# A mixture-of-experts stage: two of three f16 transposes a tile, done by DMAs from the Activation engine's queue instead of by TensorE

## The reference

```
xf = layernorm(x)
gate_scores = sigmoid(xf @ gate_w.T + balance_bias)          # 1024 tokens, 8 experts
topk_scores, topk_idx = top_k(gate_scores, 2)                # scores of the two, divided by their sum + 1e-6
h = silu(einsum('td,ehd->teh', xf, w1))                      # w1: 8 x 1024 x 512
expert_out = einsum('teh,edh->ted', h, w2)                   # w2: 8 x 512 x 1024
x = x + einsum('te,ted->td', comb, expert_out)
```

## Time and profile before

| | |
|---|---|
| median of 3 runs | 598.86 us |
| the profiled execution | 598.26 us, span 596.5 us |
| PE busy | 515.0 us, 86% |
| DVE busy | 401.4 us, 67% |
| ACT busy | 286.5 us, 48% |
| expert loop, first to last product | about 346.5 to 581.3 us of the span |
| DMA moved | 93.23 MB |

### The profile page before, as it was taken

The page is one execution under the profiler, slowest core; times in us unless marked ns, Lnnn a source line. Parts: engine busy times, 40 slices in busy tenths (PEclk is TensorE's granted clock), DMA queues, the critical chain, the costliest instruction groups (busy, mean ns, idle before and its releaser), DMA issues.

```text
span 596.5 us, 11365 instructions
## 1 busy us (share of the span) xinstructions
PE 515.0 (86%) x3769; PEld 304.1 (51%) x3770; DVE 401.4 (67%) x897; ACT 286.5 (48%) x449; POOL 114.8 (19%) x89
## 2 busy tenths in 40 slices
PE   5799999999989799886712799999999999999993
PEld 2674657475656576745401344554545555545451
DVE  2789778937978879688886656674664736673330
ACT  0662868676258374666610344562445426542120
POOL 1212114102241120300670011112111211121112
PEclk9889999999999999896855799999999999999997
DMA  8992505000008993144495157766472754623112
GB/s 320 391 382 75 213 1 212 2 1 2 1 1 324 381 381 132 37 142 142 177 316 200 46 199 210 231 185 196 123 240 36 243 145 132 220 53 53 35 35 35
DMA packets 32785, 93.23 MB, mean 156 GB/s; under 512 B 2896, under 2 KB 4080, under 8 KB 28656
## 3 DMA queue, kind: packets, MB, share of 16 engines
q1 hardware_dynamic: 23984, 74.81, 34.9%
q0 software_dynamic: 4304, 9.77, 8.2%
q10 hardware_dynamic: 4464, 8.22, 4.4%
HBM read 63.36 MB, written 29.43 MB: 156 GB/s over the span
## 4 chain that ended last, share of the span: by engine, by line
PE 67%; DVE 10%; issue 10%; ACT 5%; POOL 3%; DMA 3%; SPq 0%; ACTq 0%; POOLq 0%; DVEq 0%
PE bank L688 19%; PE bank L706 18%; PE bank L343 8%; PE bank L511 4%; PE bank L495 2%; PE bank L425 2%; PE bank L361 2%; PE bank L455 2%; PE bank L405 2%; PE bank L476 1%; PE bank L545 1%; ACT ctxT_region L736 1%; POOL small L1527 1%; DMA routed_rows<-shared,ints 1%; PE bank L604 1%
## 5 line engine op out<-in xcount | busy, mean ns | idle before, releaser
L688 PE MATMUL bank<-wbuf,ctx_region 128*128 x504 | 117.5, 392 | 6.5 <-issue 5.4
L1625 POOL DMA_INDIRECT out<-misc,ints x21 | 40.3, 1919 | 237.4 <-ACT misc L956 177.2
L688 PEld LDWEIGHTS bank<-wbuf,ctx_region 128*128 128x128 f16 x504 | 49.3, 100 | 66.9 <-issue 15.3
L1387 DVE SCALAR_TENSOR_TENSOR wbuf<-ctx_region,wbuf 128x2048 f32 (+1 forms) x28 | 62.9, 2288 | 25.9 <-ACT wbuf L875 25.9
L875 ACT ACTIVATE wbuf<-ctx_region 128x2048 f32 (+1 forms) x28 | 51.9, 1902 | 27.4 <-issue 25.6
L1527 POOL TENSOR_TENSOR small<-small 128x2 f32<-128x2 f32 (+2 forms) x25 | 27.7, 1109 | 189.2 <-DVE small L1017 182.6
L963 ACT ACTIVATE ctxT_region<-bank 128x512 f32<-128x512 f32 x42 | 25.1, 597 | 78.3 <-PE bank L688 78.3
L706 PE MATMUL bank<-wbuf,actT 128*128 x264 | 58.8, 379 | 1.0 <-DVE actT L1488 1.0
L706 PE MATMUL bank<-wbuf,xn 128*128 x240 | 53.4, 379 | 0.0
L511 PE MATMUL bank<-ctx_region,wbuf 128*128 128x256 f16 x384 | 43.3, 273 | 4.3 <-DVE ctx_region L1146 3.4
L1475 DVE COPY ints<-ctx_region 128x1 int32<-128x1 int32 x22 | 3.4, 154 | 61.0 <-PE bank L343 61.0
(11 more groups left out here) (214 smaller groups left out, 872.3 us busy)
## 6 DMA issues: line engine op xcount, KB each, us to landing
ctx_region<-in_experts SPq DMA_DIRECT2D x28, 1024.0 KB, 5.2
routed_rows<-ctxT_region SPq DMA_DIRECT2D x1, 16900.0 KB, 50.5
ctx_region<-in_ctx SPq DMA_DIRECT2D x8, 1536.0 KB, 9.1
ctx_region<-routed_rows ACTq DMA_DIRECT2D x23, 260.0 KB, 2.7
wbuf<-in_experts SPq DMA_DIRECT2D x4, 1024.0 KB, 4.8
out<-x ACTq DMA_DIRECT2D x8, 256.0 KB, 2.6
x<-in_x SPq DMA_DIRECT2D x1, 1536.0 KB, 14.5
wbuf<-in_wqT SPq DMA_DIRECT2D x4, 256.0 KB, 4.4
```

What stands on the lines that cost most here:

```text
L688: mm = nc.tensor.matmul(bank[half][:, :], xgT[:, b, x_part, k * P:(k + 1) * P], w16[:, ds(at + (w_part + k * EH + half * 512), 512)], star ...
L1387: nc.vector.scalar_tensor_tensor(w16[:, ds(at + (LOW + n * PIECE), PIECE)], src_[:, piece], W_SCALE, w16[:, ds(at + (HIGH + n * PIECE), PI ...
L1625: nc.gpsimd.indirect_dma_start(out, bass.IndirectOffsetOnAxis(idx[:, slot_no:slot_no + 1].bitcast(U32), axis=0), y_out[:, slot_no, :], Non ...
```

## The change

The rows of all tiles but the first, and the high hidden part of every tile, are transposed by DMAs with `transpose=True` from ACT's queue. Each takes 128 x 1024 f16 numbers (256 KB) from SBUF to SBUF, in eight blocks of 128 x 128. The low hidden part, and the rows of tile 0, stay on PE. PE's transposes of the rest go, with DVE's copy of the rows and ACT's copy of the high hidden part. New places and waits: ACT issues the DMA for the rows of tile u + 1 at the head of tile u, after a wait that its own rows have landed; it issues the DMA for the high hidden part right behind the two Silus, ahead of the weight cuts, after a wait for DVE's `h_hi`. DVE waits, before it writes the high part of a tile, until that of the tile before has landed in its transposed form (`hT0`).

```
 # PE
-            rows_T(0, 16)
-            first_product(0, 0, experts_of(0)[0])
-            rows_T(1, 16)
+            first_rows_T()
+            first_product(0, 0, experts_of(0)[0], first=True)
             hidden_T(0)
...
                     for u in (1, 2):
                         first_product(i * 2 + u, u % 2, experts[u])
-                        rows_T((u + 1) % 2, i * 16 + 32)
                         second_product(i * 2 + (u - 1), (u - 1) % 2, experts[u - 1])
                         hidden_T(i * 2 + u)
...
             def hidden_T(tile):
-                for part, cut, done in ((0, s["h_hi"], s["hT_ps0"]), (1, s["h_lo"], s["hT_ps1"])):
-                    pe.wait_ge(cut, tile + 1)
-                    transposes(bank[2 + part][:, :].bitcast(F16), [h16[:, part, k * P:(k + 1) * P] for k in range(HC)], done, ident16)
+                pe.wait_ge(s["h_lo"], tile + 1)
+                transposes(bank[3][:, :].bitcast(F16), [h16[:, 1, k * P:(k + 1) * P] for k in range(HC)], s["hT_ps1"], ident16)
 # ACT
+            def rows_T(b, landed):
+                act.wait_ge(xg_in[b], landed)
+                act.sem_inc(s["turning"], 1)
+                act.dma_start(xgT[:, b].rearrange("p a d -> p (a d)").rearrange("p (c t) -> p c t", t=P),
+                              xg16[:, b, 0:2 * D], transpose=True).then_inc(s["xgT"], 16)
+            def hidden(tile, b, landed, first=False):
+                if first:
+                    act.wait_ge(s["xgT0"], 1)
+                else:
+                    act.wait_ge(s["xgT"], tile * 16)
+                rows_T(1 - b, landed)
                 act.wait_ge(s["fields"], tile * 2 + 2)
                 load_rows(tile + 2, b)
...
-            def hidden_copy(tile, b):
-                act.wait_ge(s["hT_ps0"], tile + 1)
-                nc.scalar.copy(hT[b][:, 0, :], bank[2][:, :].bitcast(F16)).then_inc(s["hT0"], 1)
+            def hidden_T(tile, b):
+                act.wait_ge(s["h_hi"], tile + 1)
+                act.sem_inc(s["turning"], 1)
+                act.dma_start(hT[b][:, 0, :].rearrange("p (c t) -> p c t", t=P), h16[:, 0, :], transpose=True).then_inc(s["hT0"], 16)
...
                     for u in (1, 2):
-                        hidden(i * 2 + u, u % 2)
+                        hidden(i * 2 + u, u % 2, i * 16 + 32)
+                        hidden_T(i * 2 + u, u % 2)
                         cut_next_high(i * 2 + (u - 1), (2, 3))
                         cut_next_high(i * 2 + u, (0, 1))
-                        hidden_copy(i * 2 + u, u % 2)
                         gated(i * 2 + (u - 1), (u - 1) % 2)
 # DVE
-            def rows_copy(tile, b, again=True):
+            def rows_fields(tile, b, landed, again=True):
                 if again:
                     dve.wait_ge(s["idx"], tile - 1)
-                dve.wait_ge(s["xgT_ps"], tile + 1)
+                dve.wait_ge(xg_in[b], landed)
...
-                nc.vector.tensor_copy(xgT[:, b].rearrange("p a d -> p (a d)"), bank[(4, 7)[b]][:, :].bitcast(F16)).then_inc(s["xgT"], 1)
...
-            def cut_hidden(tile):
+            def cut_hidden(tile, again=True):
                 dve.wait_ge(s["h"], tile * 2 + 2)
+                if again:
+                    dve.wait_ge(s["hT0"], tile * 16)
                 nc.vector.tensor_copy(h16[:, 0, :], h).then_inc(s["h_hi"], 1)
```

More of the change, by code:

```diff
@@ L80 @@
 route rt_sel rt_cnt_ps rt_exp rt_slots rt_map zrow_fill zrow xs_zero rows_set scattered
-xg_in0 xg_in1 fields xgT_ps xgT h_ps h h_hi h_lo hT_ps0 hT_ps1 hT0 hT1 y2_ps y2 gate_parts gate idx scat added out_spare
+xg_in0 xg_in1 fields xgT_ps xgT0 xgT turning h_ps h h_hi h_lo hT_ps1 hT0 hT1 y2_ps y2 gate_parts gate idx scat added out_spare
 ident16 finished staged w_hi w1_lo w2_lo""".split()
@@ L668, in _, with first_rows_T @@
             pe.wait_ge(s["ident16"], 1)
-            def rows_T(b, landed):
-                pe.wait_ge(xg_in[b], landed)
-                transposes(bank[(4, 7)[b]][:, :].bitcast(F16), [xg16[:, b, k * P:(k + 1) * P] for k in range(2 * KC)],
+            def first_rows_T():
+                pe.wait_ge(xg_in[0], 16)
+                transposes(bank[4][:, :].bitcast(F16), [xg16[:, 0, k * P:(k + 1) * P] for k in range(2 * KC)],
                            s["xgT_ps"], ident16)
@@ L679, in experts_of, with first_product @@
                 return [(ready, ready % 2 * (2 * EXPERT)) for ready in (packed % 16, packed // 16 % 16, packed // 256)]
-            def first_product(tile, b, expert):
+            def first_product(tile, b, expert, first=False):
                 ready, at = expert
                 pe.wait_ge(s["w1_lo"], ready * 2)
-                pe.wait_ge(s["xgT"], tile + 1)
+                if first:
+                    pe.wait_ge(s["xgT0"], 1)
+                else:
+                    pe.wait_ge(s["xgT"], tile * 16)
                 for half in range(2):
@@ L701, in second_product @@
                 pe.wait_ge(s["w2_lo"], ready * 2)
-                pe.wait_ge(s["hT0"], tile + 1)
+                pe.wait_ge(s["hT0"], tile * 16 + 16)
                 pe.wait_ge(s["hT1"], tile + 1)
@@ L956, in gated @@
                 nc.scalar.activation(y_out[:, b, :], bank[5 + b][:, :], ACT.Copy, scale=gates[:, b, 2:3]).then_inc(s["y2"], 1)
-            def hidden(tile, b):
+            def rows_T(b, landed):
[4 more added lines that the diff above has]
+            def hidden(tile, b, landed, first=False):
+                if first:
+                    act.wait_ge(s["xgT0"], 1)
+                else:
+                    act.wait_ge(s["xgT"], tile * 16)
+                rows_T(1 - b, landed)
                 act.wait_ge(s["fields"], tile * 2 + 2)
@@ L980, in _ @@
             load_rows(1, 1)
-            hidden(0, 0)
-            hidden_copy(0, 0)
+            hidden(0, 0, 16, first=True)
+            hidden_T(0, 0)
             act.wait_ge(s["w2_lo"], 2)
@@ L1469, in cut_next_low, with first_rows_copy @@
                     cut_low(stage, at * -1 + 2 * EXPERT, pieces, ready * W_PIECES)
-            def rows_copy(tile, b, again=True):
+            def rows_fields(tile, b, landed, again=True):
                 if again:
                     dve.wait_ge(s["idx"], tile - 1)
-                dve.wait_ge(s["xgT_ps"], tile + 1)
+                dve.wait_ge(xg_in[b], landed)
                 nc.vector.tensor_copy(tokens[:, b:b + 1], xg[:, b, C_TOKEN:C_TOKEN + 1].bitcast(I32)).then_inc(s["fields"], 1)
                 nc.vector.tensor_copy(fields[:, b, :], xg[:, b, C_G1:C_E2 + 1]).then_inc(s["fields"], 1)
-                nc.vector.tensor_copy(xgT[:, b].rearrange("p a d -> p (a d)"), bank[(4, 7)[b]][:, :].bitcast(F16)).then_inc(s["xgT"], 1)
-            def cut_hidden(tile):
+            def first_rows_copy():
+                dve.wait_ge(s["xgT_ps"], 1)
+                nc.vector.tensor_copy(xgT[:, 0].rearrange("p a d -> p (a d)"), bank[4][:, :].bitcast(F16)).then_inc(s["xgT0"], 1)
+            def cut_hidden(tile, again=True):
                 dve.wait_ge(s["h"], tile * 2 + 2)
+                if again:
+                    dve.wait_ge(s["hT0"], tile * 16)
                 nc.vector.tensor_copy(h16[:, 0, :], h).then_inc(s["h_hi"], 1)
@@ L1503, in _ @@
             cut_low(expert0, 2 * EXPERT, (0, 1), 0)
-            rows_copy(0, 0, again=False)
+            first_rows_copy()
+            rows_fields(0, 0, 16, again=False)
             cut_low(expert0, 2 * EXPERT, (2, 3), 0)
-            rows_copy(1, 1, again=False)
-            cut_hidden(0)
+            rows_fields(1, 1, 16, again=False)
+            cut_hidden(0, again=False)
             hidden_copy(0, 0)
@@ L1514, in _ @@
                     for u in (1, 2):
-                        rows_copy(i * 2 + (u + 1), (u + 1) % 2)
+                        rows_fields(i * 2 + (u + 1), (u + 1) % 2, i * 16 + 32)
                         cut_hidden(i * 2 + u)
```

## The result

The changed kernel took 619.64 us (median of four runs, 617.79 to 630.49) beside 599.01 us (598.34 to 600.0) of the kernel before: a ratio of 1.033, with a 95% interval from 1.030 to 1.037. The forecast of 612 us had the direction right and was 7.6 us short; the time lies in the range of 590 to 690.

What follows compares the result with a forecast made beforehand. PE was taken to bound the expert loop end to end. Removing 23.5 us gave 575.4 us; 13 cut tiles at 0.8 + T, with T = 2.0, brought 612 us, 2% slower, range 590 to 690.

Steps and rivals of the forecast that it cites:

- What goes: PE, loop and ahead of it: row transposes 9.0, high hidden part 8.9, start 0.6, branch gap 5.0; 23.5 us less.
- The mechanism of the loss: ACT's queue in cut tiles: cast wait and DMA issue delay weight cuts, DVE's low copy and PE; 0.8 + T each.
- the formula: Total time: 575.4 + 13 x (0.8 + T) us, over the 13 of 20 tiles with weight cuts.
- T: Time one transposing DMA holds ACT's queue: taken as 2.0 us, range 0.34 to 5.3.
- Transfers: no cost: DMA engines in the loop: half busy, so two transposing DMAs a tile, 0.9 to 1.8 us each, fit at no cost.
- the third rival: Transposing DMAs fill all 16 DMA engines, up to 687 us; decides above 3.3 us each; chance 0.08.
- PE waits for the transfers themselves: Sign in the loop's changed profile that would show the predicted mechanism wrong; no size given.
- PE's clock at full: PE during the loop's new waits: full clock assumed, nothing added; a granted clock below 1 would add to them.
- Short issue: ACT's queue: the DMA's hold is short, 590 us at 0.34 us, faster below 1.0 us; chance 0.16.
- stronger form: ACT's table loads pass the wait for the cast, so all 23.5 us come, 575 us; chance 0.07.
- Long issue: ACT's queue bounds every tile when the hold exceeds 3.15 us; 685 us at 5.3; chance 0.17.
- Full DMA engines: Transposing DMAs keep all 16 engines 5.2 us each, 16.4 us a tile, 687 us; chance 0.08.

Runs made afterwards that it cites:

- E3: Changed kernel with only the rows transposed by DMA, both hidden parts on PE as before, old order on ACT: 588.32 us, ratio 0.988.
- E1: Changed kernel with the high hidden part's DMA issued behind ACT's table loads and weight cuts instead of ahead: 582.58 us, ratio 0.976.
- E9: E1 with only ACT's wait for DVE's cast put back ahead of the table loads and cuts: 592.5 us, ratio 0.990.
- E2: Changed kernel with both transposing DMAs as plain copies of the same bytes, same waits, expert outputs not the reference's: 598.47 us, ratio 1.0005.
- E4: Changed kernel with only the high hidden part by DMA, ahead of the cuts, rows back on PE and DVE: 615.65 us, ratio 1.035.
- E8: Changed kernel with each 1 MB weight piece loaded by four DMAs of 256 KB: 613.57 us, ratio 1.026.
- E10: Changed kernel with the high hidden part's DMA split into two of 128 x 512, both ahead of the cuts: 626.59 us, ratio 1.050.
- E6: E1 with the low hidden part also transposed by a DMA behind the cuts: 577.42 us, ratio 0.966.

## Why the prediction was right, and where it was not

**What goes: right.** Tiles without cuts run at 10.81 us, the forecast's 10.8; the gap at the branch closed; and E3, in which nothing new bound, came out at 588.3 us, where its half of the forecast gives 589.3. Ahead of the loop the forecast had 0.6 us, and about half of it came: from the start of the stage's first product to that of the next it took 13.39 us (324.82 to 338.21), now 13.12 (326.24 to 339.36). DVE's cast does follow the Silu at once now, but PE's idle time of the reason "issue" ahead of that product rose from 1.68 us to 2.04. And the first product began 1.4 us later in the profiled run, which was not in the sum.

**The mechanism of the loss: right.** The wait for the cast, the table loads that lose their cover, the cuts, DVE's copy: E1 undoes it and gains 35 to 37 us, E9 shows the wait's share, and E9, E2 and the changed kernel show the formula's slope in T. Its constant of 0.8 measured 1.07; ACT's cut began 3.11 us behind the DMA in the tile shown, where 2.88 was put in.

**T: mis-sized.** Taken as 2.0, it measured 1.27. The value was chosen midway between a plain issue's 1.20 and a backlogged queue's 2.92; the lower neighbour was nearly exact. With 1.27 the forecast's own formula gives 575.4 + 13 x 2.07 = 602.3 us.

**"Transfers: no cost": the step that failed.** It rested on plain transfers. Queue 10 and the packets of the loop, before and then after (345 to 600 us; packets, MB, share of 16 engines):

```profile
q10 hardware_dynamic: 2736, 5.06, 6.7%
```

```profile
DMA packets 49420, 44.44 MB, mean 174 GB/s; under 512 B 41589, under 2 KB 41589, under 8 KB 46453
q10 hardware_dynamic: 43333, 15.15, 37.6%
q1 hardware_dynamic: 3347, 24.27, 31.5%
```

The 39 transposing DMAs of that stretch added 10.1 MB in 40,600 packets, some 250 bytes each. They took 30.9% of 255 us, 2.0 us of all engines apiece: only just over the 1.8 that I had as the upper bound, and far from the 3.3 at which the third rival decides. The room had been read off a mean. The DMA share of the kernel before was 0.50 over the loop, but 0.68 in the first five cut tiles and 0.23 behind the last one; the changed kernel reaches 1.13 in a cut tile (same columns as above, before and then after):

```profile
345.00:408.00 63.00, 62.15 (x383) 31.95 (x382) 43.22 (x65) 32.69 (x31) 10.60 (x5) 1.00 0.68 211
536.00:580.00 44.00, 43.57 (x273) 22.52 (x272) 14.77 (x37) 9.22 (x15) 4.94 (x4) 1.00 0.23 42
```

```profile
526.00:537.00 11.00, 9.40 (x51) 4.39 (x50) 6.37 (x8) 5.48 (x5) 2.63 (x1) 1.00 1.13 193
```

Nor had I asked how long one takes to land beside weight loads: 3.1 us at best, up to 15.3. Three second products waited for one, 10.6 us, and "PE waits for the transfers themselves" was a sign that I had named of a wrong mechanism: it holds for these three of the thirteen waits. DVE's cast waited for the same three landings, 7.8 us, where the prediction saw about 9 us of room.

**PE's clock at full: the second step that failed.** Three second products in the PE timeline,

```profile
360.61 7.04 PE L708 MATMUL bank<-wbuf,xn 128*128 x24 [2.40 <-DVE xn L1507]
...
376.43 8.28 PE L708 MATMUL bank<-wbuf,actT 128*128 x24 [3.16 <-DMA actT<-ctxT_region]
...
421.12 8.12 PE L708 MATMUL bank<-wbuf,xn 128*128 x24 [6.41 <-DMA xn<-ctxT_region]
```

took 7.4 us more than three of 5.35, at a mean granted clock of 0.77, 0.62 and 0.64 in their windows (the two levels are 1.0, which is 2.4 GHz, and 0.5); the prediction named this and put it at nothing. PE had stood idle for 2.4, 3.2 and 6.4 us before them. It is no matter of landings alone: 1.7 of the 7.4 us stand behind a wait for DVE, and in E4 and E8, where no product waits for a landing, all of the 7.9 and 9.5 us do. Other waits of that size were not followed by it, as the one of 3.52 us above.

The account of the profiled execution, 620.3 us: 575.4; thirteen waits 34.3; lower clock 7.4; later start 1.4; 1.8 is not accounted for, of which some 0.3 is what did not come ahead of the loop. Against the formula at the measured T (602.3), the waits for DVE were 3.0 longer (10 x 0.3), the three for landings 4.4 longer than three times 2.07, and the rest as above: 18.0. So two errors of opposite sign, 9.5 us too much for T and 18 too little for landings, clock and start, gave 612. The hit is better than its reasons.

**The rivals.** Short issue: refuted by T, though its point of decision, T = 1.0, was only 0.27 us away. Its stronger form, loads that pass the wait: refuted by the 7.92 us of ACT's idle time. Long issue: refuted, 2.07 us was the longest in the changed kernel. Full DMA engines: refuted as a bound on every tile, by 2.0 us apiece where it needed 3.3 and by a pace of 10.81 us in tiles without cuts. In cut tiles it was not far off, as the share of 1.13 shows. Of the two pages that I set against each other: the figure of 1309 ns for a 128 x 128 block ("VectorE: DVE Perf Modes", "The three transpose paths", in the Trainium skill; the page gives it for bf16, not for f16) does not add up over blocks here, for eight f16 blocks land in 3.1 us at best. The other page ("Advanced Engine Details and Errata", "X-Bar Transpose (TRN2)", in the Trainium skill) says that transposing DMAs are as fast as regular ones. That does not carry over to what binds here: the queue is held 1.27 us against 0.48 for the same copy in E2, and in the loop only the transposing form made PE wait for a landing.

## What to carry to other kernels

Moving work off the bounding engine is half a change; the other half is where in the new engine's in-order queue its wait and its issue stand. Put them behind the work that others wait for (E1: one line, some 36 us), and count the hold per DMA, not per block (E10). Before calling a transfer free, ask when it must land and what else is then in the DMA engines, in the very tiles in which it must land; a mean share over the stage (0.50 here) doesn't tell. And where a change makes PE wait, price the clock too: in E8 slow products cost 9.5 us beside waits of 29.3.

## What the runs showed of the hardware

- In the changed kernel a transposing DMA of 128 x 1024 f16 from SBUF to SBUF held ACT's queue 1.26 to 1.29 us (medians). One of 128 x 512 held it 1.29 to 1.30 (E10), a plain copy of 128 x 1024 0.48 (E2), a plain row load from DRAM 0.35. Issued right behind another one, it held it 2.2 to 2.3 (E6).
- It moves in packets of about 250 bytes, lands in 3.1 us at best and in up to 15.3 beside 1 MB weight loads, in up to 8.9 beside the same loads cut in four (E8).
- In a cut tile of the changed kernel the DMA engines moved 193 GB/s at a share of 1.13 (526 to 537 us); the weight and context loads of the kernel before moved 386 GB/s at 1.04 (23 to 42 us). So with the small packets the engines were as full at half the bytes.
- While ACT computed, its queue issued the DMA behind (E1, 501.71 within the cut of 500.58, which lasts until 502.49); the next cut still began at 502.39, so this hold did not delay ACT.
- Behind waits of 2.3 to 6.4 us second products ran in part at the lower clock level, 6.8 to 8.3 us for 5.35, whatever PE had waited for (E4, E8, the changed kernel); behind others of 2.6 to 3.5 us they did not.
